# Two networks of experts on one core: first product and gelu over halves of 4 sequences, and the last network's first product in plain fp32 for the two units of 2 sequences

## The reference

```
x1 = x  + cross attention to the context (77 positions)
x2 = x1 + norm(x1) + 0.3 * mixture(mla(norm(x1)))      # 16 heads; 8 experts, the best 2 weighted by `combine`
         h1 = gelu(mla @ w1[e] + b1[e])                # 128 -> 256, for every expert e
         h2 = h1 @ w2[e] + b2[e]                       # 256 -> 128
x3 = x2 + second cross attention of norm(x2) (context again), with W_qv of 4 x 128 rows
y  = x3 + p7 * (gelu(norm(x3) @ W1[7] + b1[7]) @ W2[7] + b2[7])   # 128 -> 512 -> 128, router weight p7
```

## Time and profile before

| | |
|---|---|
| median of 3 runs | 160.07 us (159.89 to 160.13) |
| the profiled execution's own time | 160.33 us |
| its span, first to last instruction | 158.5 us |
| experts' stage, from `m1:1,0,0` to the end of `m2:2,7` | 94.89 to 130.66 us |
| last store issued, by the first core's SyncE | 156.3 us |

### The profile page before, as it was taken

How to read it: one execution, slowest core, us unless ns; L and a number is a source line. 1 busy time by engine, 2 the same in 40 slices (tenths; PEclk the granted TensorE clock), 3 DMA queues, 4 the chain that set the end, 5 groups by cost and what they waited for, 6 DMA issues and landing times.

```text
span 158.5 us, 3986 instructions
## 1 busy us (share of the span) xinstructions
PE 146.0 (92%) x1288; PEld 118.0 (74%) x1296; DVE 109.3 (69%) x413; ACT 105.9 (67%) x238; POOL 50.5 (32%) x155
## 2 busy tenths in 40 slices
...
PEclk9999999999999999999999999999999999999999
...
GB/s 100 156 76 271 203 2 0 149 115 74 113 155 181 104 50 54 19 2 4 35 0 4 0 0 0 4 0 2 0 4 0 2 6 0 0 0 2 4 67 65
DMA packets 11072, 8.03 MB, mean 51 GB/s; under 512 B 1867, under 2 KB 10155, under 8 KB 11051
## 3 DMA queue, kind: packets, MB, share of 16 engines
...
...
## 4 chain that ended last, share of the span: by engine, by line
PE 49%; issue 21%; DVE 14%; ACT 7%; POOL 4%; DMA 2%; ACTq 1%; SPq 1%; POOLq 1%; DVEq 0%
PE ps L1098 47%; DVE qbd L876 2%; DVE nmax L882 2%; DMA x<-in_x_dram 2%; POOL rstd L571 2%; DVE stats L784 1%; DVE xn L799 1%; ACT pr L631 1%; ACT pexp L662 1%; POOL xn L565 1%; ACTq L58 1%; ACT L727 1%; DVE mv L788 1%; ACT mT L655 1%; DVE res L851 1%
## 5 line engine op out<-in xcount | busy, mean ns | idle before, releaser
L712 ACT ACTIVATE vpad<-ps,b1o 128x256 f32<-128x256 f32 (+1 forms) x48 | 23.3, 543 | 17.3 <-PE ps L1098 17.1
L1098 PE MATMUL ps<-w2s,vpad 128*128 128x128 f32 x256 | 32.4, 276 | 0.0
L1098 PEld LDWEIGHTS ps<-w2s,vpad 128*128 128x128 f32 x256 | 30.4, 192 | 0.8 <-issue 0.2
L995 DVE SCALAR_TENSOR_TENSOR vpad<-ps,comb,vpad 128x128 f32<-128x128 f32 x64 | 18.4, 343 | 10.3 <-PE ps L1098 10.1
L882 DVE TENSOR_REDUCE nmax<-ps 128x4 f32<-128x512 f32 x32 | 20.9, 685 | 5.5 <-PE ps L1098 5.4
L662 ACT ACTIVATE pexp<-ps 128x512 f32<-128x512 f32 x32 | 18.2, 594 | 2.5 <-PE ps L1098 1.9
L1098 PE MATMUL ps<-ao,w_lo 128*128 128x256 f32 (+1 forms) x48 | 16.4, 356 | 0.8 <-ACT vpad L712 0.8
L1098 PE MATMUL ps<-ao,w_hi 128*128 128x256 f32 (+1 forms) x48 | 14.6, 318 | 0.0
L565 POOL TENSOR_TENSOR xn<-vpad,bqv 128x256 f32<-128x256 f32 (+1 forms) x3 | 2.7, 915 | 36.5 <-DVE vpad L995 36.5
L571 POOL TENSOR_TENSOR rstd<-veps,power 128x2 f32<-128x2 f32 (+1 forms) x6 | 4.8, 808 | 28.2 <-DVE veps L794 28.2
L1098 PE MATMUL ps<-kst,qbd 128*128 128x128 bf16 x128 | 11.8, 219 | 2.1 <-DVE nmax L882 2.1
...
## 6 DMA issues: line engine op xcount, KB each, us to landing
...
```

The costliest lines, as they stand in the source:

```text
L712: act.activation(hT[:, k % 2, c, 0:n], ps[:, h1_bank(k, c), 0:n], ACT.Gelu, bias=b1o[:, e, c:c + 1]).then_inc(s["gelu_ok"], 1)
L995: dve.scalar_tensor_tensor(out=x2[:, a + i, :], in0=ps[:, 2 + k % 2, i * D:(i + 1) * D], scalar=comb[:, a + i, e:e + 1], in1=x2[:, a + i, ...
L1098: return nc.tensor.matmul(dst, lhsT, rhs, start=start, stop=stop)
```

## The change

Units 1 and 2 share one first product and gelu: `m1:1,e,c` now covers sequences 4 to 7 (512 columns), and `m1:2,*` and `gelu:2,*` are gone. The gelus of this half go into a tile `hT1` that holds all eight experts, in the memory of `qbd` (so the trace will call it `qbd`), and no longer wait for `h2_ps`. `m2` and `acc` stay in units of 2 sequences. `p5_f1` stays `split3` for unit 0; for units 1 and 2 it is one plain fp32 matmul straight from `f1s` and `x4T`, without `x4_hi` and `x4_lo`. The output of the last gelu moves to the memory of `kst` (unit 0) and `w1s` (units 1, 2). The whole table `plan` is another one.

```diff
-        gT = qbd[:, 0:GROUPS // 2, :, :].rearrange(...).bitcast(FP32).rearrange("p (c t) -> p c t", c=F1)
+        hT1 = qbd[:, :, :, :].rearrange("p g j t -> p (g j t)").bitcast(FP32).rearrange("p (e c t) -> p e c t", e=E0, c=F0)
...
-            if k % 2 == 0 or k >= 2 * E0:
+            if k % 2 == 0:
                 return c
...
             def gelu0(u, e):
-                k, n = u * E0 + e, UNITS[u][1] * S
+                k = u * E0 + e
                 for c in range(F0):
                     act.wait_ge(s["h1_ps"], F0 * k + c + 1)
-                    if k >= 2:
+                    if u == 0 and k >= 2:
                         act.wait_ge(s["h2_ps"], k - 1)
...
-                    act.activation(hT[:, k % 2, c, 0:n], ps[:, h1_bank(k, c), 0:n], ACT.Gelu,
+                    act.activation(hT1[:, e, c, :] if u else hT[:, k % 2, c, :], ps[:, h1_bank(k, c), :], ACT.Gelu,
...
                 act.activation(x4T[:, toks(u)], v, ACT.Copy).then_inc(s["xT3_ok"], 1)
-                act.activation(x4_hi[:, toks(u)], v, ACT.Copy).then_inc(s["x4hi_ok"], 1)
+                if u == 0:
+                    act.activation(x4_hi[:, toks(u)], v, ACT.Copy).then_inc(s["x4hi_ok"], 1)
...
-                    pe.wait_ge(s["gelu_ok"], F0 * (k - (2 if k <= 2 * E0 else 1)) + c + 1)
+                    pe.wait_ge(s["gelu_ok"], F0 * (k - 2) + c + 1)
...
-                split3(ps[:, (bank_a, bank_b)[c % 2][u], 0:UNITS[u][1] * S], f1_hi[:, f], f1_lo[:, f],
-                       x4_hi[:, toks(u)], x4_lo[:, toks(u)]).then_inc(s["f1_ps"], 1)
+                dst = ps[:, (bank_a, bank_b)[c % 2][u], 0:UNITS[u][1] * S]
+                if u == 0:
+                    last = split3(dst, f1_hi[:, f], f1_lo[:, f], x4_hi[:, toks(u)], x4_lo[:, toks(u)])
+                else:
+                    last = mm(dst, f1s[:, f], x4T[:, toks(u)])
+                last.then_inc(s["f1_ps"], 1)
...
-            m1:1,1,1 m2:1,0 gelu:1,4 m1:1,2,0 m1:1,2,1 acc:0,6 m1:1,3,0 m1:1,3,1 acc:0,7 m2:1,1 acc:1,0 p4_ln:0 m2:1,2 acc:1,1
+            gelu:1,2 m1:1,1,1 fw1 gelu:1,3 acc:0,7 m1:1,2,0 gelu:1,4 m1:1,2,1 m1:1,3,0 p4_ln:0 m1:1,3,1 acc:1,0 m1:1,4,0 acc:1,1
```

More of the change, by code:

```diff
@@ L297, in build @@
         plan = stages_of("""
[L298 to L305, removed]
@@ L318, in build @@
-            m1:1,1,1 m2:1,0 gelu:1,4 m1:1,2,0 m1:1,2,1 acc:0,6 m1:1,3,0 m1:1,3,1 acc:0,7 m2:1,1 acc:1,0 p4_ln:0 m2:1,2 acc:1,1
-            m1:1,4,0 m1:1,4,1 x2b:1 m1:1,5,0 m1:1,5,1 m2:1,3 acc:1,2 p4_T:0 m2:1,4 gelu:1,5 p4_norm:0 gelu:1,6 p4_sim:0 m1:1,6,0
-            m1:1,6,1 m1:1,7,0 acc:1,3 m2:1,5 m1:1,7,1 m1:2,0,0 acc:1,4 m2:1,6 p4_simd:0 m1:2,0,1 acc:1,5 gelu:1,7 m1:2,1,0 acc:1,6
-            p4_mx:0 m2:1,7 p4_nbm:0 gelu:2,0 p4_exp:0 gelu:2,1 p4_probs:0 m2:2,0 m1:2,1,1 acc:1,7 p4_pT:0 gelu:2,2 m1:2,2,0
@@ L322, in build @@
-            m1:2,2,1 acc:2,0 fw1 p4_ln:1 m2:2,1 p4_hq:0 p4_norm:1 m1:2,3,0 m1:2,3,1 m2:2,2 p4_hh:0 acc:2,1 m1:2,4,0 m1:2,4,1
-            gelu:2,3 acc:2,2 gelu:2,4 p4_outd:0 gelu:2,5 p4_T:1 p5_ln:0 acc:2,3 p4_out:0 m2:2,3 m1:2,5,0 acc:2,4 gelu:2,6
-            p4_simd:1 m1:2,5,1 m2:2,4 acc:2,5 p4_exp:1 gelu:2,7 p4_nbm:1 p5_norm:0 m1:2,6,0 m1:2,6,1 p4_sim:1 m2:2,5 p4_probs:1
-            p4_mx:1 m1:2,7,0 m1:2,7,1 p5_T:0 m2:2,6 acc:2,6 acc:2,7 p4_pT:1 m2:2,7 p5_router:0 p4_hh:1 p4_ln:2 p4_hq:1 p5_f1:0,0
@@ L326, in build @@
-            p4_norm:2 p5_f1:0,1 p4_outd:1 p4_out:1 p5_f1:0,2 p4_T:2 p5_ln:1 p5_f1:0,3 p4_sim:2 p4_simd:2 x2b:2 p5_norm:1 p5_exp:0
-            p4_nbm:2 p5_f2:0,0 p4_mx:2 p4_exp:2 p4_probs:2 p5_f2:0,1 p5_prob:0 p4_pT:2 p5_T:1 p4_hq:2 p4_hh:2 p5_f2:0,2
-            p5_router:1 p4_outd:2 p5_exp:1 p4_out:2 p5_f1:1,0 p5_ln:2 p5_norm:2 p5_f1:1,1 p5_f2:0,3 p5_f1:1,2 p5_f1:1,3 p5_T:2
-            p5_prob:1 p5_f2:1,0 p5_router:2 p5_end:0 p5_end:1 p5_f1:2,0 p5_prob:2 p5_f1:2,1 p5_f1:2,2 p5_f1:2,3 p5_f2:1,1
```

86 lines of the change are left out of this document (58 added, 28 removed).

## The result

The changed kernel takes 159.37 us (median of 20 runs), the kernel before, run beside it, 160.91 us (20 runs). The ratio is 0.9913, 95% interval 0.9889 to 0.9937: about 0.9% faster. The profiled execution took 158.49 us, the fastest of the twenty, with a span of 156.7 us, where before it was 160.33 and 158.5. The forecast was 157.9 us and 1.3%: the direction is right, the size of the gain is not.

What follows compares the result with a forecast made beforehand. TensorE's queue was taken to bound the kernel to about 147 us, then the last unit's serial chain. 160.33 - 0.5 (early) - 1.8 (second half) + 0.15 (tail) = 158.2, less 0.26 for the median: 157.9 us; range 156.6 to 159.5.

Steps and rivals of the forecast that it cites:

- Groups: Units 1 and 2 on TensorE: some 15 groups of `m1` become 5, 10 x 0.09 = 0.9 us less.
- the 0.3 us for unit 0: Unit 0's experts, ahead of `m1:1,0,0`: they come in fewer groups, 0.3 us less by the same 0.09.
- Gelu waits: Unit 2's `m1`: two waits of TensorE for a gelu vanish with four banks, 1.1 us less, 0 back.
- The late chain: Unit 0's layer norm 3, between `p4_out:0` and `p5_T:0`: 1.9 us new waiting against 1.4 before, 0.5 us back, bounds 0 to 1.5.
- The rest of 0.3 us: `m1:1,0,0` to `p4_sim:2`: two short waits at `p4_mx:0` and `p4_pT:0` covered by an `m2`, 0.3 us less.
- Ahead of `m1:1,0,0`: Front, attention and unit 0's experts in a new order: 0.5 us less, bounds -1.2 and +0.2.
- the front: First stages, where `p1_av:1` now precedes `setup`: order effects taken to cancel, 0, open by 0.70 us either way.
- `p5_f1` and the tail: Last unit's end: plain fp32 products 0.2 us later, little removed on that path; 0.15 us more, bounds -0.4 and +0.6.
- Table loads: ScalarE: one pair of loads, 2 x 1.28 us, goes and is not waited for; 0, at worst 0.6 us more.
- A: Rival: late chain at unit 0's norm 3 costs its upper bound, the front brings nothing; 159.3 us, chance 0.15.
- C: Rival: unit 1 finishes 1.9 us later and its chain sets the end; slower, 161.6 us, chance 0.08.
- Up to about 147 us it is the amount of work: Whole kernel: TensorE's queue and its fixed order's waits limit until about 147 us, then the last unit's serial chain.

Runs made afterwards that it cites:

- e6: Changed kernel plus ten filler matmuls, results unread, in TensorE's idle gap before `s1:0,2`; 158.73 us, ratio 0.9880 to the kernel before.
- e7: Kernel before plus the same ten filler matmuls before `s1:0,2`; 160.31 us, ratio 0.9967 to the kernel before.
- e12: Changed kernel with ten filler matmuls, its run of eight `m1` cut by `m2` into pairs, seven groups in place of five; 158.94 us, ratio 0.9895.
- e11: Changed kernel with ten filler matmuls, `m1` of the second half given one pair of PSUM banks in place of two; 161.61 us, ratio 1.0063.
- e3: Kernel before with the new order only for front, attention and unit 0's experts, ahead of `m1:1,0,0`; 159.95 us, ratio 0.9942.
- e15: Kernel before with ten filler matmuls and only the front, up to `rows:0`, in the new order; 160.04 us, ratio 0.9964 to the kernel before.
- e2: Changed kernel with `split3` put back for `p5_f1` of units 1 and 2; 159.42 us, ratio 0.9919 to the kernel before.
- e1: Kernel before with only `p5_f1` of units 1 and 2 made one plain fp32 matmul; 160.59 us, ratio 1.0001.

## Why the prediction was right in its direction and wrong in its size

**The number it was measured against.** The three runs shown gave 160.07 us; twenty gave 160.91, since 46 of the 100 executions of the kernel before with a clock on record lose about 1 us to the clock. At a mean clock of 0.995 and more it takes 160.33 us (54 executions) and the changed kernel 159.08 (16): 1.2 us less, where 2.2 were forecast. The spans of these executions fell by 1.5 us, from 158.5 to 157.0 (medians); 0.3 us of that is lost outside the span, and the runs don't show why. With fillers in both kernels it is 1.6 us (e6, e7). The profiled executions differ by 1.84 us; the sum for that one was 158.2, and it took 158.49, but it is the fastest of its twenty, so that this agreement is in part luck.

**Groups: the step that failed.** "10 x 0.09 = 0.9 us less" was read from one side only. The row of the first `m1` behind an `m2` shows the 0.09; that the `m2` in front of it is shorter by as much could be read by comparing `m2` followed by `m1` (97.71 to 98.52 in the earlier trace rows, 0.81) with a pair of them (1.70 us, from the row below to 97.15, in the kernel before). e12 measures 0.015 us a group in the changed kernel, so 0.15 us for the ten. The same error stands in the 0.3 us for unit 0, where the traces show 0.06.

```profile
95.45 1.95 PE L1098 MATMUL ps<-w2s,vpad 128*128 128x128 f32 x16
```

**Gelu waits.** The forecast was 1.1 us less and 0 back. The waits were there, as rows of the kernel before on either side of them show:

```profile
108.53 0.28 PE L1098 MATMUL ps<-ao,w_hi 128*128 128x256 f32 x1
...
112.60 0.66 PE L1409 MATMUL ps<-ident,pr 128*77 128x128 f32 x4
```

From 108.53 to the `m1` at 109.28 it is 0.63 us more than the 0.12 of such a matmul, and from 112.60 to the one at 113.55 it is 0.45 more than the 0.50 that these transposes take in the changed kernel: 1.08 us. In the changed kernel the run of eight has no idle time, and e11 shows that waits for a gelu go to the end in full. No run takes away these two waits alone, but the stage's sum closes with them: 0.15 + 1.1 - 0.1 = 1.15, measured 1.14.

**The late chain.** The place was right. The new waiting is 1.5 us in place of 1.9, so 0.1 comes back and not 0.5, if the 1.4 us of waiting before the change stands. Two estimates were off. The chain from the end of `p4_out:0` to the last norm takes 4.9 us (120.50 to 125.41) and not 5.2, since between the variance and the norms pass 1.4 us (122.92 to 124.28) and not 1.6. And TensorE's work beside it is 3.3 us and not 3.1, because an `m2` ahead of other plain fp32 work costs 0.90 us and not 0.81, the same oversight as in the groups.

**The rest of 0.3 us** that the walk gave has no counterpart in the trace: the short waits at `p4_mx:0` and `p4_pT:0` are still there, 0.25 us in all as before. With groups and chain corrected nothing is left for it.

**Ahead of `m1:1,0,0`.** -0.83 us in the two traces shown, about -0.6 between the middles of all traces of either order, -0.4 in e3's executions, and -0.5 forecast: the size was right. The parts were not those forecast: unit 0's groups brought 0.06 (taken as 0.3), and the front (taken as 0) and the attention (taken as 0.2) the rest, the front perhaps 0.3 by e15. That the sum came out is luck.

**`p5_f1` and the tail.** +0.17 us against +0.15, but not for the reason given: with `split3` kept the new tail is 0.18 us longer still (e2), while in the old order the plain product costs 0.32 (e1). So the +0.17 belongs to the new order of the tail, and that the term came out is luck. The two plain products at 143.08 take 1.03 us together, 0.43 from start to start, as forecast. The Trainium skill ("FP8 and Floating Point Precision", TensorE Precision Notes) gives four passes for true fp32; by it the prediction's 0.107 us for a pass over 256 columns would make 0.43, and this trace agrees.

**Table loads.** One pair less, and not waited for: `p5_f1:0` was not delayed. Cost 0, as taken.

**The rivals.** A (159.3 us) is nearest in time, but not by its mechanism: the late chain cost less than forecast, not its upper bound, and the early order brought something. C did not come: `p4_T:1` at 120.50 follows TensorE's work without a wait. "Up to about 147 us it is the amount of work" was wrong too: in the changed kernel the chain that ended last waits on VectorE and ScalarE from 135.8 us on, though no term hung on it.
